# A mixture-of-experts stage on one core: the down product moved between the halves of the third product

## The reference

```python
x = layernorm(x).reshape(-1, H)
logits = SOFTCAP * jnp.tanh(x @ w_gate / SOFTCAP)
probs = jax.nn.softmax(logits, axis=-1)
_, idx = jax.lax.top_k(probs, TOPK)
weights = probs * one_hot(idx).sum(-2)
for e in range(E):
    h = silu(x @ w1[e]) * (x @ w3[e])
    out = out + h @ w2[e] * weights[:, e:e+1]
```

## Time and the profile before

| what | value |
|---|---|
| median of 3 runs | 699.2 us (697.81 to 699.62) |
| the profiled execution, device time | 698.2 us |
| its span in the trace | 696.4 us |
| TensorE busy over the span | 638.3 us, 92% |
| steps 5 to 20 (597.17 to 680.05 us) | 82.88 us, TensorE busy all of it |

### The profile page before, as it was taken

The page is one execution under the profiler, slowest core; times in us unless marked ns, Lnnn a source line. Parts: engine busy times, 40 slices in busy tenths (PEclk is TensorE's granted clock), DMA queues, the critical chain, the costliest instruction groups (busy, mean ns, idle before and its releaser), DMA issues. The chain is left out here.

```text
span 696.4 us, 14843 instructions
## 1 busy us (share of the span) xinstructions
PE 638.3 (92%) x4509; PEld 584.2 (84%) x4510; DVE 600.1 (86%) x1386; ACT 549.8 (79%) x1927; POOL 463.8 (67%) x646
## 2 busy tenths in 40 slices
PE   1579999999999999999999999999998479999994
PEld 0578899999999999999999999999977457888883
DVE  7797899999989999998999999888898877777771
ACT  5787889998998999999899999988875245666670
POOL 4777777688677768867786886787565425454532
PEclk9989999999999999999999999999999669999998
DMA  7101100020020102002000110200099412323232
GB/s 224 61 1 57 36 1 31 2 61 32 1 62 2 32 1 62 32 1 62 1 32 1 54 42 2 62 2 1 1 355 341 159 31 49 52 53 53 46 45 23
DMA packets 35509, 37.72 MB, mean 54 GB/s; under 512 B 2704, under 2 KB 30352, under 8 KB 35440
## 3 DMA queue, kind: packets, MB, share of 16 engines
q1 hardware_dynamic: 31024, 30.84, 13.3%
q0 software_dynamic: 4416, 6.03, 5.4%
HBM read 31.62 MB, written 5.24 MB: 53 GB/s over the span
## 5 line engine op out<-in xcount | busy, mean ns | idle before, releaser
L1459 POOL TENSOR_SCALAR shared<-shared,rsum 128x256 f32<-128x256 f32 x256 | 143.8, 573 | 56.1 <-DVE rsum L1004 51.0
L707 ACT ACTIVATE shared<-s,nmax 128x256 f32<-128x256 f32 x256 | 122.2, 498 | 22.9 <-DVE nmax L999 22.7
L1453 POOL TENSOR_TENSOR rstd<-rstd,half 128x7 f32<-128x7 f32 (+1 forms) x64 | 88.8, 1387 | 5.3
L999 DVE TENSOR_REDUCE nmax<-s 128x2 f32<-128x512 f32 x128 | 86.7, 680 | 3.1 <-PE s L380 3.0
L1009 DVE TENSOR_TENSOR pt_lo<-t,pt_hi 128x512 fp32r<-128x512 f32 x124 | 84.2, 679 | 1.9 <-ACT pt_hi L715 0.9
L715 ACT CAST pt_hi<-t 128x512 fp32r<-128x512 f32 x124 | 74.1, 597 | 9.8 <-PE t L395 7.2
L723 ACT ACTIVATE shared<-route_bank,head_w 128x512 f32<-128x512 f32 (+1 forms) x124 | 81.5, 689 | 0.0
L395 PE MATMUL t<-ident,shared 128*128 128x128 f32 x496 | 75.3, 275 | 5.9 <-POOL shared L1459 2.7
L994 DVE TENSOR_TENSOR qk_lo<-shared,qk_hi 128x512 fp32r<-128x512 f32 x96 | 78.3, 815 | 2.4 <-POOL qk_hi L1470 1.3
L336 PE MATMUL pj_a<-w_ring,xq 128*128 128x256 f32 x488 | 72.9, 293 | 6.9 <-POOL xq L1535 6.9
L2007 DVE TENSOR_TENSOR w_lo<-expert_w,w_hi 128x1024 fp32r<-128x1024 f32 x46 | 56.2, 1224 | 25.6 <-ACT w_hi L1885 24.9
(11 more groups left out here) (275 smaller groups left out, 1929.1 us busy)
## 6 DMA issues: line engine op xcount, KB each, us to landing
expert_w<-in_w SPq DMA_DIRECT2D x24, 512.0 KB, 9.2
spare<-in_wT SPq DMA_DIRECT2D x19, 256.0 KB, 3.1
wp_raw<-in_wpT SPq DMA_DIRECT2D x16, 256.0 KB, 2.9
spare<-in_wkvT SPq DMA_DIRECT2D x16, 128.0 KB, 3.3
spare<-in_wT SPq DMA_DIRECT2D x9, 128.0 KB, 3.6
spare<-in_x SPq DMA_DIRECT2D x1, 1024.0 KB, 5.9
x_hat<-acc SPq DMA_DIRECT2D x1, 1024.0 KB, 4.6
out<-spare SPq DMA_DIRECT2D x1, 1024.0 KB, 6.9
```

The costliest lines, as they stand in the source:

```text
L707: e = act.activation(probs[:, st, h * S:(h + 1) * S], s_bank[st][:, h * S:(h + 1) * S], ACT.Exp, bias=nmax[:, st, h:h + 1], accum_out=psum ...
L999: dve.tensor_reduce(nmax[:, st, :], s_bank[st][:].rearrange("p (h t) -> p h t", h=2), AX, ALU.max, negate=True).then_inc(max_done, 1)
L1453: pool.tensor_tensor(rstd[:, st, c], rstd[:, st, c], half[:, c], ALU.pow).then_inc(rstd_ready, 1)
L1459: m = pool.tensor_scalar(probs[:, st, c], probs[:, st, c], rsum[:, st, h:h + 1], 1.0, ALU.mult, ALU.mult)
```

## The change

There are five edits, all in `experts`.

1. TensorE: the third product is cut in two halves of three matmuls (`part` 0 and 1). The down product of step n stands between the halves of the third product of slot n+1.
2. VectorE: in a step `take_y(n)` stands ahead of `take_hidden(n+1)`; it stood last before.
3. TensorE: `stay_awake` issues 10 matmuls after the slots' tokens are found and 2 after the first rows are transposed. Their output is overwritten later and read by nobody.
4. VectorE's start: the nine short instructions for `factor` and its parts are spread around the first `w_lo`; `hid` of slot 0 and the copy of the scales stand ahead of `fill_places`; `find_fill` on TensorE stands at the end of step 0, and `out_rows_known` in step 0, behind the `w_lo` of slot 2, not ahead of it.
5. GpSimd: five gathers ahead of the loop instead of four, and in the loop scatter n stands ahead of gather n+5.

```diff
             def hidden(n, par, i, part=None):
...
+                if part != 1:
+                    pe.wait_ge(w_split, 2 * n + i + 1)
                 trio = [(k, l, r) for k in range(KT) for l, r in ((xsT_hi, w13_hi), (xsT_hi, w13_lo), (xsT_lo, w13_hi))]
-                for j, (k, l, r) in enumerate(trio):
+                half = len(trio) // 2
+                for j, (k, l, r) in list(enumerate(trio))[half if part == 1 else 0:half if part == 0 else None]:
...
-                m.then_inc(h_done, 1)
+                if part != 0:
+                    m.then_inc(h_done, 1)
...
+            def stay_awake(times):
+
+                for _ in range(times):
+                    pe.matmul(h3_bank[1][:, 0:P], ident[:], acc[:, 0, 0:P], start=True, stop=True)
+
+            stay_awake(10)
             pe.wait_ge(slots_known, 1)
             turn_rows(0, 0)
+            stay_awake(2)
             hidden(0, 0, 0)
...
                 turn_hidden(n, par)
                 if more:
-                    hidden(n + 1, 1 - par, 1)
+                    hidden(n + 1, 1 - par, 1, 0)
+                if isinstance(n, int) and n == 0:
+                    pe.wait_ge(scales_known, 1)
+                    pe.wait_ge(tokens_known, 1)
+                if isinstance(n, int) and n == 1:
+                    pe.wait_ge(out_known, 1)
+                down(n, par)
+                if more:
+                    hidden(n + 1, 1 - par, 1, 1)
                 if isinstance(n, int) and n == 0:
                     find_fill()
-                    pe.wait_ge(scales_known, 1)
-                    pe.wait_ge(tokens_known, 1)
-                down(n, par)
...
                     weights_rest(n + 2, par, e, 0)
+                if isinstance(n, int) and n == 0:
+                    out_rows_known()
+                    dve.wait_ge(scales_known, 1)
+                take_y(n, par)
                 if not isinstance(n, int) or n + 1 < SLOTS:
                     take_hidden(n + 1, 1 - par)
                 if more:
                     weights_rest(n + 2, par, e, 1)
-                take_y(n, par)
...
             weights_rest(1, 1, e, 1)
+            take_hidden(0, 0)
+            dve.wait_ge(scales_found, 1)
+            dve.tensor_copy(row_scale[:], y_bank[0][:, 0:SLOTS]).then_inc(scales_known, 1)
             fill_places()
             fill_table()
-            dve.wait_ge(scales_found, 1)
-            dve.tensor_copy(row_scale[:], y_bank[0][:, 0:SLOTS]).then_inc(scales_known, 1)
-            take_hidden(0, 0)
-            out_rows_known()
-            dve.wait_ge(scales_known, 1)
             steps(dve, step)
...
-            for n in range(4):
+            for n in range(5):
                 load(n, n % 2)
             pool.wait_ge(route.sums_begun, 16)
             pool.wait_ge(out_known, 1)
             for n in range(SLOTS):
-                if n + 4 < SLOTS:
-                    load(n + 4, n % 2)
-                if n >= 1:
-                    scatter(n - 1, (n - 1) % 2)
-            scatter(SLOTS - 1, (SLOTS - 1) % 2)
+                scatter(n, n % 2)
+                if n + 5 < SLOTS:
+                    load(n + 5, (n + 1) % 2)
```

More of the change, by code:

```diff
@@ L1737, in experts @@
             sem("last_known"), sem("last_ranked"), sem("fill_known"), sem("fill_found"), sem("out_known"))
+        factored = sem("factored")
         weighed, scales_found, scales_known = sem("weighed"), sem("scales_found"), sem("scales_known")
@@ L1776, in turn_rows, with hidden @@
                 m.then_inc(xt_done, 1)
-            def hidden(n, par, i):
-                if i == 0:
+            def hidden(n, par, i, part=None):
+                if part != 1 and i == 0:
                     pe.wait_ge(xt_split, n + 1)
@@ L1784, in hidden @@
                 bk = (h1_bank, h3_bank)[i]
-                pe.wait_ge(w_split, 2 * n + i + 1)
+                if part != 1:
+                    pe.wait_ge(w_split, 2 * n + i + 1)
                 trio = [(k, l, r) for k in range(KT) for l, r in ((xsT_hi, w13_hi), (xsT_hi, w13_lo), (xsT_lo, w13_hi))]
-                for j, (k, l, r) in enumerate(trio):
+                half = len(trio) // 2
+                for j, (k, l, r) in list(enumerate(trio))[half if part == 1 else 0:half if part == 0 else None]:
                     m = pe.matmul(bk[par][:], l[:, par, k, :], r[:, par, i, k * I:(k + 1) * I],
                                   start=j == 0, stop=j == len(trio) - 1)
-                m.then_inc(h_done, 1)
+                if part != 0:
+                    m.then_inc(h_done, 1)
             def turn_hidden(n, par):
@@ L1970, in _ @@
             dve.tensor_scalar(slot_expert[:], slot_f[:], float(E - 1), None, ALU.min).then_inc(slots_known, 1)
[L1972 to L1984, removed]
             def slot_scales():
@@ L2071, in step @@
                     weights_rest(n + 2, par, e, 1)
-                take_y(n, par)
             dve.wait_ge(slots_known, 1)
             e = expert_of(0)
+            dve.wait_ge(exped, 1)
+            dve.wait_ge(route.f_gated, 1)
+            link(dve.tensor_reduce(total[:], prob[:, :, 0:E], AX, ALU.add))
+            link(dve.reciprocal(total[:], total[:]))
+            link(dve.tensor_scalar(total[:], total[:], route.fgate[:, 0:1], None, ALU.mult))
+            dve.tensor_tensor(factor[:], prob[:, :, E:E + TOP].rearrange("p t j -> p j t"),
+                              total[:].rearrange("p (o t) -> p o t", o=1).broadcast_to([P, TOP, NT]), ALU.mult).then_inc(factored, 1)
             weights_rest(0, 0, e, 0)
             weights_rest(0, 0, e, 1)
+            dve.wait_ge(factored, 1)
+            whole = factor[:].rearrange("p j t -> p (j t)")
+            link(dve.tensor_copy(factor_part[:, 0, :], whole))
+            link(dve.tensor_tensor(left[:, 0, :], whole, factor_part[:, 0, :], ALU.subtract))
+            link(dve.tensor_copy(factor_part[:, 1, :], left[:, 0, :]))
+            dve.tensor_tensor(left[:, 1, :], left[:, 0, :], factor_part[:, 1, :], ALU.subtract).then_inc(factored, 1)
             rows_rest(0, 0)
             last_rows()
+            dve.wait_ge(factored, 2)
+            link(dve.tensor_copy(factor_part[:, 2, :], left[:, 1, :]))
             slot_scales()
```

## The result

The changed kernel takes 705.06 us (median of 6 runs, 704.69 to 706.51); beside it the kernel before took 698.47 (697.76 to 699.62). The ratio is 1.0093 [1.0083, 1.0104]: slower, by some 6.6 us. The forecast was 705.5.

The account below looks back on a forecast made before the run. The prediction took TensorE, full in steps 5 to 20 at 5.18 us each, as the bound. Steps +7.6 and start -0.8 gave +6.8 on 698.2 or 699.2, so 705.5 us; 8-in-10 range 702.0 to 709.5.

Parts of the forecast that it names:

- The sum: Whole kernel: 7.6 - 0.8 = +6.8 us, giving 705.0 from 698.2 or 706.0 from 699.2; forecast 705.5.
- The mechanism in the steps: TensorE in the steps: a wait on a closed ring recurs every step, 5.56 us against 5.18; +7.6 us in all.
- Rival (a): Steps: TensorE slips 0.38 us once, then finds everything ready; 697.8 us, or 696.1 with the whole clock gain; chance 0.11.
- the signs that I had named: TensorE's steps: right if 5.5 to 5.6 us; wrong if 5.18, or 5.7 or more with the gap before y.
- First path: VectorE in the steps: the third product waits for `w_lo`, ready at E + 2.34; 0.38 us a step.
- E: Moment in a step when a third product has ended and the next matmul could start; path times count from it.
- Second path: ScalarE in the steps: y waits for the copy of `hidT` until E + 3.09; alone 0.34 us a step.
- Rival (b): Steps: the register load ahead of y is exposed on TensorE; 0.57 us a step, 11.4 in all, 708.8 us; chance 0.09.
- Putting `y_sb` ahead of `hid` does not lengthen it: VectorE in the steps: `y_sb` is over at E - 0.02 and `hid` would wait until E + 0.26 anyway.
- The start: Kernel start: unread products can bring a higher TensorE clock; between +0.4 and -2.5 us, taken as -0.8.
- Rival (c): Start: unread products do nothing for the clock; +0.4 in place of -0.8, 706.2 us; chance 0.80 together with the forecast.
- The end and GpSimd: Kernel end and GpSimd's order: end unchanged, scatters 4.60 us apart against a step of 5.56; gain nothing.

## Why the prediction was right, and where its terms were off

**The sum** came out at +6.8 and the difference is +6.6, but two terms were off by some 1.7 us each way: the steps cost 9.2 us (1.19 + 7.42 + 0.60) where I had 7.6, and the start gave 2.6 where I had 0.8. That the two misses cancelled was luck; that the kernel became slower was not.

**The mechanism in the steps** held: waits that recur in every step since they hang on TensorE's own progress. Rival (a), waits paid once, is out: 5.675 us for each of 15 steps. By the signs that I had named, this lies between right (5.5 to 5.6) and wrong (5.7 or more with the gap ahead of y), and the larger gap is ahead of y, which I had named as the sign of the copy or the register load.

**First path.** I took `w_lo` to be ready at E + 2.34. The rows of the changed kernel sum to less: `hid` at E + 0.20 and 0.26, `w_lo` 0.61 behind it and not 0.70, the product 0.05 behind its end and not 0.15, so E + 2.08 and E + 2.14. The wait is 0.11 to 0.17 us, not 0.38.

**Second path.** Here the sentence "Each step costs the larger, 0.38" failed, in which path is the larger one. I had the load of y at E + 2.99; it is at E + 3.05 and E + 3.26. In the one step the copy starts at E + 2.25, as I had it, and the load follows its end by 0.21 instead of 0.15. In the other, ScalarE idles 0.55 ahead of `w_hi`, where I read 0.32 off one step of the trace of before. `w_hi` ends late, and the copy behind it starts 0.77 after ht instead of 0.64; the load follows by 0.29. The mean of the two steps, 5.58 and 5.79, is the 5.68 of the table.

The trace of before had this already. The step of the earlier trace rows and of the 0.32 is step 20, which is written out behind the loop. In the loop ScalarE idles 0.40 and 0.56 by turns, and in step 5 the copy starts 0.77 after ht there too:

```profile
598.44 1.05 ACT L1885 CAST w_hi<-expert_w 128x1024 fp32r x1 [0.56 <-issue]
598.63 0.60 PE L1797 MATMUL ht_bank<-ident,hid 128*128 128x128 f32 x4
599.40 0.58 ACT L1909 COPY hidT<-ht_bank 128x512 f32<-128x512 f32 x1
```

In the kernel before it cost nothing, since the weight load of y came at 600.23, behind the whole third product and 0.25 after the copy's end. The run with `w_lo` first shows that the first path was not the binding one: without its wait the step is 5.647.

**Rival (b)**, a register load ahead of y that TensorE feels, stays partly open. The load follows the copy by 0.21 to 0.29 us where 0.15 was read, so at most 0.06 to 0.14 us a step can be its share; no run takes it away. With the cut after five matmuls it does not show: y's weight load starts at 650.08, with the fifth h matmul. Its 0.57 a step was too much.

**"Putting `y_sb` ahead of `hid` does not lengthen it"** held in the changed kernel (`hid` at E + 0.20), but with no room: `y_sb` ends at 660.13 and `hid` starts at 660.14, where I had it over at E - 0.02. With the cut after five matmuls, or with the down product put back, `y_sb` becomes the path.

**The start.** I took -0.8, since the clock might not stay; the end of -2.5 was the better one. Rival (c), unread products without effect, is out: without them 2.1 of the 2.6 us are gone, and the 0.5 that stays is that of the other edits. The trace has the clock at 1.00 from 561.50 on, with the transposes and two of the unread products ahead of slot 0's first product. By the Trainium skill's rule on transposes ("TensorE: Matmul & The Clock Gate", Part 4: PE-mode transpose) I had worked out a start worth nothing. What the transposes did to hold the clock, no run here shows; in the old order of the start two products behind them did not hold it and eight did.

**The end and GpSimd.** "Gain: nothing" fits the changed kernel, whose step of 5.68 us is longer than the scatters' chain; GpSimd's order of before was not run in it. I had taken 4.60 us between scatters from the last two, when no gather runs between them. In the run with GpSimd's order of before they are 5.18 apart on the mean, and at a step as long edit 5 is worth some 3 us (24.67 - 21.53).

**What is best.** The version with edits 3 to 5 alone: 695.13 us against 698.63 beside it.

## What to carry to other kernels

When two engines both feed the bound one, write down the closed ring through each, and read the durations in several steps of the loop itself: one read from a step written out behind the loop (0.32 us) was 0.40 and 0.56 by turns inside it. Where rings of almost the same length stand side by side, a single remedy may show nothing; try them together before dropping either. And a chain of transfers that wait for each other, as long as a step, is a second bound: here it cost nothing until the compute started sooner, and then took the whole gain.

## What the runs showed of the hardware that was not expected

In the kernel before with unread products the granted clock had risen to 1.00 and was 0.56 again once TensorE had idled 1.47 us; in the changed kernel an idle time of 1.05 us at the same place left it at 1.00. One execution of each was profiled, and that the length of the idle time decides was not tested. One indirect DMA of 128 rows out of `y_sb` occupied GpSimd for 1.62 us on the mean in the version without edits 1 and 2, and for 2.08 in the same version with GpSimd's order of before; the kernel before, in that order too, has 1.65.
